# Causal mask of the attention exponents: small matmuls into the scores for every head, in place of selects on GpSimd

## What is computed

```python
x = _layernorm(x)                       # then q, k, v = x @ W + b, split in 16 heads of 8
scores = jnp.einsum('bthd,bshd->bhts', q, k) / jnp.sqrt(8)
scores = scores + slopes[:, None, None] * -abs(kpos - qpos)
scores = jnp.where(causal, -jnp.inf, scores)        # causal: key after query
attn = jax.nn.softmax(scores, axis=-1)
out = jnp.einsum('bhts,bshd->bthd', attn, v)        # then @ Wo + bo, added to x
```

## Time and profile before

| | us |
|---|---|
| median of 3 runs (lowest, highest) | 837.1 (834.55, 839.06) |
| the profiled execution, its own time | 835.53 |
| its span in the profile | 833.8 |
| attention stage in it, first S step to last O | 120.3 to 534.0 |
| busy in the span: PE, DVE, ACT, POOL | 660.7, 514.9, 449.1, 153.6 |

### The profile page before, as it was taken

How to read it: one execution, slowest core, us unless ns; L and a number is a source line. 1 busy time by engine, 2 the same in 40 slices (tenths; PEclk the granted TensorE clock), 3 DMA queues, 4 the chain that set the end, 5 groups by cost and what they waited for, 6 DMA issues and landing times.

```text
span 833.8 us, 14733 instructions
## 1 busy us (share of the span) xinstructions
PE 660.7 (79%) x5478; PEld 313.6 (38%) x5478; DVE 514.9 (62%) x1024; ACT 449.1 (54%) x765; POOL 153.6 (18%) x245
## 2 busy tenths in 40 slices
PE   3730168989998988898989987477499999999963
PEld 2420023333333333332333322146345666666642
DVE  5970287889888888888888883066502433344433
ACT  2940016877878877778777788404133334443321
POOL 2650041222212222211222122111000000000000
PEclk9885559999999999999999999877589999999986
DMA  9887550221123220121210300100000000000001
GB/s 177 202 203 200 157 136 5 44 47 29 25 45 74 46 48 24 29 72 46 48 32 22 74 7 9 30 6 1 0 1 1 1 13 15 13 2 13 13 13 26
DMA packets 49806, 40.58 MB, mean 49 GB/s; under 512 B 9772, under 2 KB 44724, under 8 KB 49724
## 3 DMA queue, kind: packets, MB, share of 16 engines
q1 hardware_dynamic: 43576, 37.22, 19.5%
q10 hardware_dynamic: 6160, 2.43, 1.2%
HBM read 22.32 MB, written 17.04 MB: 47 GB/s over the span
## 4 chain that ended last, share of the span: by engine, by line
PE 59%; DVE 14%; ACT 6%; issue 4%; POOL 2%; DMA 1%; SPq 0%; POOLq 0%; DVEq 0%; ACTq 0%
PE sums L761 14%; DVE neg_max L787 10%; PE ring L740 9%; PE ring L1277 8%; PE ring L1268 7%; PE bank L712 5%; ACT probs L808 5%; PE ring L1269 2%; PE bank L706 2%; PE ring L1281 1%; PE bank L1314 1%; PE bank L1217 1%; PE bank L1325 1%; DMA denominators<-weighted_sums 1%; PE ring L723 1%
## 5 line engine op out<-in xcount | busy, mean ns | idle before, releaser
L787 DVE TENSOR_REDUCE neg_max<-bank 128x2 f32<-128x1024 f32 (+2 forms) x320 | 342.7, 1115 | 62.7 <-PE bank L712 61.0
L808 ACT ACTIVATE probs<-ring 128x512 f32<-128x512 f32 (+4 forms) x481 | 302.0, 681 | 80.0 <-PE ring L740 65.9
L712 PE MATMUL bank<-k_operand,q_operand 54*128 54x512 bf16 (+3 forms) x768 | 144.7, 339 | 48.2 <-PEq L369 46.4
L740 PE MATMUL ring<-q_operand,k_operand 56*128 56x512 bf16 (+3 forms) x768 | 164.4, 333 | 17.9 <-ACT probs L808 14.3
L761 PE MATMUL sums<-probs,v_all 128*9 128x512 f32 (+3 forms) x1536 | 162.4, 495 | 2.7 <-POOL probs L840 2.1
L840 POOL TENSOR_SCALAR_AFFINE_SELECT probs<-probs 128x512 f32<-128x512 f32 x128 | 80.1, 634 | 225.0 <-ACT probs L808 224.2
L740 PEld LDWEIGHTS ring<-q_operand,k_operand 56*128 56x128 bf16 x768 | 50.3, 94 | 152.2 <-ACT probs L808 110.2
L1385 ACT ACTIVATE hid<-ring,b1c 128x512 f32<-128x512 f32 x64 | 44.0, 687 | 81.8 <-PE ring L1269 81.3
L706 PE MATMUL bank<-masks 64*128 64x128 bf16 (+2 forms) x768 | 72.1, 224 | 5.2 <-DVE neg_max L787 4.9
L1277 PE MATMUL ring<-w,hid 128*128 128x128 f32 x512 | 74.8, 290 | 0.0
L712 PEld LDWEIGHTS bank<-k_operand,q_operand 54*128 54x128 bf16 x768 | 46.0, 97 | 65.6 <-issue 47.7
(11 more groups left out here) (151 smaller groups left out, 647.9 us busy)
## 6 DMA issues: line engine op xcount, KB each, us to landing
q_rows<-qk_parts SPq DMA_DIRECT2D x48, 128.0 KB, 2.4
k_rows<-qk_parts SPq DMA_DIRECT2D x48, 128.0 KB, 2.4
q_operand<-q_rows SPq DMA_DIRECT2D x64, 96.0 KB, 3.3
k_operand<-k_rows SPq DMA_DIRECT2D x32, 192.0 KB, 3.9
weighted_sums<-osum SPq DMA_DIRECT2D x128, 18.0 KB
sums_in<-in_L_attn_x SPq DMA_DIRECT2D x4, 512.0 KB, 7.4
x_res<-in_L_attn_x SPq DMA_DIRECT2D x4, 512.0 KB, 14.3
q_operand<-max_rows_sb SPq DMA_DIRECT2D x128, 2.0 KB
```

The source lines that it names most:

```text
L712: last = nc.tensor.matmul(ps[:, h, w * j:w * j + w], q_op[rows, buf, t // CH, p, P * (t % CH):P * (t % CH) + P], k_op[rows, buf, p, CW * k ...
L740: last = nc.tensor.matmul(psS[:, bank, w * j:w * j + w], k_op[rows, buf, p, P * kb:P * kb + P], q_op[rows, buf, c, p, q0:q0 + w], start=Tr ...
L787: nc.vector.tensor_reduce(neg_max[:, n % 2, slot, kc, :, pairs[0]:pairs[-1] + 1, t % CH], src, AX.X, ALU.max, negate=True).then_inc(a_read, 1)
L808: nc.scalar.activation(dst, src, ACT.Exp).then_inc(ring_read, 1)
```

## The change

The selects on POOL and the semaphore `masked` go away; every diagonal S step adds the pair of mask matmuls for every head; and in the planner a diagonal S costs 150 ns more instead of 60, M no longer exists, and a diagonal unit's V may stand 60 ns after its exponents. The list `ORDER` is made anew from these costs, so the order of all steps may differ.

```diff
-    SEM, DRAIN, COPY, CUT, HOP, MASK = 60, 170, 260, 500, 2600, 660
+    SEM, DRAIN, COPY, CUT, HOP = 60, 170, 260, 500, 2600
...
-            pe = start + max(len(pairs) for _, pairs in heads) * stream(w) + (60 if UNITS[u][5] else 0)
+            pe = start + max(len(pairs) for _, pairs in heads) * stream(w) + (150 if UNITS[u][5] else 0)
...
-                if UNITS[u][5]:
-                    order.append(("M", n, u))
-                    pool = max(pool, act + SEM) + MASK
-                    probs_done[n, u] = pool + SEM
...
-                            guard = diag and 2.0 ** (-8.0 / H * (GH * (n % NBUF) + 2 * h + p + 1)) * (P - 1) > 40
                             last = nc.tensor.matmul(psS[:, bank, w * j:w * j + w],
                                                     k_op[rows, buf, p, P * kb:P * kb + P],
-                                                    q_op[rows, buf, c, p, q0:q0 + w], start=True, stop=not guard)
-                            if guard:
+                                                    q_op[rows, buf, c, p, q0:q0 + w], start=True, stop=not diag)
+                            if diag:
                                 both = slice(64 * h, 64 * h + 64)
                                 nc.tensor.matmul(psS[:, bank, w * j:w * j + 64], masks[both, 0, 0, :],
                                                  masks[both, 2, 0, 0:64], start=False, stop=False)
...
-                    if diag:
-                        pe.wait_ge(masked, n * len(DIAG) + DIAG.index(u) + 1)
...
-                def mask(n, u):
-
-                    pool.wait_ge(ring_read, EXPS_END[n, u])
-                    tri = probs[:, u % NPROBS, :, :, 0:P].rearrange("p h j q -> p (h j) q")
-                    nc.gpsimd.affine_select(out=tri, in_=tri, compare_op=ALU.is_ge, fill=0.0, base=0,
-                                            pattern=[[0, GH], [1, P]], channel_multiplier=-1).then_inc(masked, 1)
...
-                    if kind == "M":
-                        mask(n, *args)
-                    elif kind == "F":
+                    if kind == "F":
```

More of the change, by code:

```diff
@@ L120 @@
 LAST = [max(u for u in range(NU) if UNITS[u][0] == s) for s in range(QC)]
-DIAG = [u for u in range(NU) if UNITS[u][5]]
 MAXUNITS = max_units()
@@ L634, in build @@
             cut_chain, cut_ready, low_ready = sem("cut_chain"), sem("cut_ready"), sem("low_ready")
-            o_clear, masked, pv_done, o_ready = (sem(n) for n in ("o_clear", "masked", "pv_done", "o_ready"))
+            o_clear, pv_done, o_ready = (sem(n) for n in ("o_clear", "pv_done", "o_ready"))
             NMIN = 2 * MAXROWS
```

## The result

The changed kernel takes 856.86 us (median of 4 runs, 856.46 to 857.19) against 835.83 us of the kernel before (4 runs, 834.21 to 839.06), a ratio of 1.0246 with a 95% interval of 1.0212 to 1.0281. It is slower by 21 us. The forecast was slower by 11 us, 848 us, with a range of 832 to 860.

The account below looks back on a forecast made before the run. No engine was saturated: PE, DVE and ACT were close, with handovers between them. Terms 7.1 + 4.8 - 0.5 + 0 gave +11.4 us, on the 837.1 us median 848.5, stated as 848 us, range 832 to 860.

Parts of the forecast that it names:

- Three more heads in 12 groups: Attention groups without guards: 24 added mask pairs cost 0.59 us each group, +7.1 us in all (bounds 6.1 and 13.4).
- The fourth head: All 16 attention groups: eight added mask pairs cost 0.3 us each group, +4.8 us in all (bounds 0 and 11.5).
- The selects and the wait: Removing POOL's selects and the wait on them: nothing in steady groups, -0.5 us at the end (bounds -1.1 and +0.5).
- The new order: PE's remade list of steps in the attention stage: taken as 0 us, with bounds of -14 and +12 us.
- B: Rival: the added mask work hides in PE's idle time in each group; about 837 us, chance 0.13.
- C: Rival: no added mask pair is covered on PE, each counts in full; 862 us, chance 0.10.
- A: Rival: the new list drops T steps that wait, up to 1.2 us per steady group; 834 or 841 us, chance 0.22.
- The Trainium skill's rate: About 81 ns per 128-column matmul on PE, so 67 us for the 416 added pairs, 904 us; 1 in 100.
- What was to be seen in the profile: Signs: unguarded groups 26.1 to 26.2 us, PE busy 24.0, T waits below 1.5, selects gone, attention ending 11 us later.

Follow-up runs that it names:

- e3: The kernel before with mask pairs for the first three heads in all 16 groups, selects kept; ratio 1.0067 to the kernel before.
- e1: The kernel before with its list of steps kept, mask pairs for all heads and no selects; ratio 1.0098 to the kernel before.
- e4: The kernel before without selects or the wait for them, no pairs added, so most heads' triangles stay unmasked; ratio 0.9928 to the kernel before.
- e6: The kernel before with the planner's cost of cutting the maxima at 1400 ns instead of 500, so T steps stand later; 819.28 us, ratio 0.978.
- e12: The kernel before with up to two neighbour swaps per group, putting half-row scores steps ahead of V steps; ratio 1.0134 to the kernel before.

## Why the prediction was right or wrong

**Three more heads in 12 groups, +7.1 us: right.** e3 gives 0.61 us to a group against the 0.59 read from groups 8 and 12.

**The fourth head, 0.3 us to a group: right in kind, too small.** It is 0.42 us in the old list and 0.63 in the changed kernel's.

**The selects and the wait, nothing in the steady groups: right; -0.5 us at the end: too small.** The last group falls by 3.0 us without masks, by 2.0 us with pairs (e1, 22.06 us) and by 3.4 us in the changed kernel. I had summed two waits that the timeline puts down to the select, 0.33 and 0.77 us. The same group has a third, 0.41 us at 519.44, that I missed, and a stretch at the lower clock, worth about 1.3 us, that I didn't look for. I had put the 1.38 us that ACT waits for the scores down to PE's work as such; in e4, with the same scores and sums at the full clock, the wait is 0.20 us:

```profile
527.10 1.41 ACT L806 ACTIVATE probs<-ring 128x384 f32<-128x384 f32 x2 [0.20 <-PE ring L740]
```

**The new order, 0: this step failed.** It costs 11.9 us: the stage ends 22.3 us later in the changed kernel and 10.4 us later in e1, and the times above the kernel before differ by as much (21.0 and 9.2 us). Up to 1.8 us of it may be the one dip of the clock in group 10. I had written that the same A, T, S and V steps have to fit and that the long parts of the cycle aren't touched. Both are true, and still the order decides, since PE's own time depends on who stands beside whom: a step of one half of the rows cost 0.00 us beside a step of both halves and 0.30 us ahead of a V. My bounds for it, -14 and +12 us, did hold the truth, at the upper end; but the upper bound came from a T step placed 1 us too early, which is not what happened. So that the range held the time is in part luck. I had looked for the edit's harm or gain at the T steps, where the waits can be seen, and not in PE's busy time, where the loss went: it grew by 2.30 us in a steady group, 0.65 more than the pairs add in the old list.

**Rivals.** B (hidden) is refuted by e1. C (nothing is covered) came near in time, 862, for the wrong reason: the pairs are covered in part, only 1.03 of 1.65 us of busy time lengthen the group. A is a true mechanism that this edit doesn't set off: it drops no waiting T step (1.2 us of waiting is left), and the edit that does, e6, gives what A promised. The Trainium skill's rate of about 81 ns to each matmul of 128 columns ("TensorE: Matmul & The Clock Gate", section "Back-to-back issue gap") would have given 67 us; the measured price of a pair of matmuls in place is 1.03 / 32 = 32 ns of kernel time and 1.65 / 32 = 52 ns of PE's busy time. This case does not bear the rate out for matmuls of half the rows.

**What was to be seen in the profile.** Selects and waits for POOL before the sums gone, the steady groups alike but for the dip in group 10, waiting before T below 1.5 us, later stages the same: as said. Groups of 26.1 to 26.2 us and PE busy for 24.0: not so in the changed kernel (26.96, 24.89) but nearly so with the old list (26.28, 24.24).

## What to carry to other kernels

Where a planner writes the order of the work, an edit of its costs is a second change, to be measured apart: here it cost as much as the new instructions. A group of the trace that already does what the edit will do everywhere can price it well: here to 0.02 us to a group, as long as the list stayed the same. And work moved from an idle engine to the busiest one paid only where that one idled: of the whole change, the last group alone was worth it.

## What the runs showed of the hardware that was not expected

Matmuls of the two halves of PE's rows can start within 10 ns of each other when they stand beside one another in the queue (both at 362.21 in the kernel before), and the same step of 512 columns costs 0.00 us or 0.30 us of PE's time by its neighbour alone. At most two swaps of neighbours in a group made the kernel 1.3% slower (e12), one constant in the planner 2.2% faster (e6), with not one instruction added or removed.

The price of 32 pairs was 1.03 us in the old list and 1.04 in the one with late T steps, though PE's idle time and its busy time differ between the two. What sets that share is open.

In the last group PE's granted clock fell in all four profiles with selects and no pairs there (0.86 to 0.93 in the mean of the group) and in none of the ten others. Eight records of the sums then took 1.90 us in place of 1.05.
